# Row factors of the t and s operands as one-hot products on turned columns, in the last stage of a three-stage kernel

## The chip, the cores and the metric

One core of a Trainium2 chip runs the whole program. Times are device microseconds of one execution. The kernel before took 1745.47 us (median of three runs, 1743.71 to 1745.48). TensorE does the matmuls, VectorE (DVE), ScalarE (ACT) and GpSimd (POOL) the elementwise work; SyncE (SP), ScalarE and GpSimd issue DMAs.

## What is computed

Attention-like mixing and a gated MLP come first; they give x1, 4096 tokens of 512 channels. The change lies in the third stage, which conditions each token by table rows and sends it through two layers and a quantised product:

```python
h = _ln(x, pw_g[pathway_ids], pw_b[pathway_ids])
h = _ln(h, cp_g[compartment_ids], cp_b[compartment_ids])
t = _ln(x, tm_g[time_steps], tm_b[time_steps])
m = x + _mlp_ln(memory_state, ...)[:, None, :]      # n and r alike
s = _ln(x, ms_g[scale_type], ms_b[scale_type])
cat = concatenate([w[0]*h, w[1]*t, w[2]*m, w[3]*n, w[4]*r, w[5]*s])
u = _mlp_ln(cat, int_W1, int_b1, int_W2, int_b2, int_g, int_be)
x = x + quantised_product(u, rhs)                   # int8 rows and columns
```

`_ln(x, g, b)` is the layer norm of a token times g plus b. tm_g has 5 rows and ms_g has 3, of 512 channels each; pw_g has 500. The shifts tm_b, ms_b and cp_b and the vectors of m, n and r are already brought in by a small table, `bias_t`, multiplied by a one-hot matrix of the tokens' ids.

## The kernel before

`conditioned_ffn` holds the stage. It runs over eight blocks of 512 tokens (TT = 4 tiles of 128). In each, the first layer is a sum over 16 steps: four steps x (the columns of x1, channel-major, loaded from `x1T_d`), four steps h, then t and s in turn for the four channel groups k. `main(b, s)` on TensorE multiplies four blocks of weights by one operand of 128 channels x 512 tokens, in three passes over high and low parts: 12 matmuls a step (L2085; the last four steps are `main_last`, L2112). The operand's high part is made by ScalarE (`front_high`, L2293, or `x_high`, L2286, for x), its low part by VectorE (`front_low`, L2711), in four slots `op`.

For h, t and s the operand comes from token-major tiles. For t and s a table row per token (`ts_rows`, 1024 numbers) is gathered by GpSimd with an indirect DMA (`gather_ts`, L2537) into `gts`. ScalarE writes the centred x1 into `xh` (`x_centre`, L2302). VectorE multiplies the t half by xh (`t_product`, L2701) and GpSimd the s half (`scale_rows`, L2544). TensorE turns the products, four transposes an operand (L2048), into one bank of a ring of four, and ScalarE and VectorE take their parts from the bank. For h the same is done with `hn`: rows gathered from pw_gb (L2518), multiplied and added on GpSimd (`h_rows`, L2557, L2559), moments on VectorE, rstd and shift on GpSimd (`rsqrt`, L2548, L2550), centring on ScalarE, and a product with cp_rows on VectorE (`h_product`, L2696).

The order on each engine is written out by hand:

- TensorE: the list `order` puts the items (turned operands, q products) between the main steps; then `main_last`; then `second(b)` (L2133), the second layer. `wait_bank` waits until the bank's last content has been read. main(b + 1, 0) waits for `take_u` to have emptied the accumulators.
- ScalarE: 16 steps, then `hidden(b)` (L2361, L2364), then the x operands of the next block. `h_centre(b + 1, [0, 1])` stands in step 15, before `hidden(b)`.
- VectorE: `steps_of(b)` begins with the moments of u of block b - 1; in its steps stand the moments of x and h of block b + 1, `scale` and `clip` of block b - 1 and front_low. Then `hidden(b)` (L2717), front_low of x steps 0 and 1, `h_product(b + 1)`, `take_u(b)` (L2735, waits for each result of the second layer), front_low of x steps 2 and 3.
- GpSimd: `body(b)`: scale_rows(b), two gathers of pw rows, rsqrt of u, `tail_gain(b - 1)` (L2579, L2581: u times a row plus a row), `tokens(b + 1)` (rsqrt of x, h_rows, four gathers of cp_rows, rsqrt of h), tail_add of tiles 0 and 1 (L2587), gather_ts, tail_add of tiles 2 and 3.
- SP: ids, residual rows, the turns of q by DMA, the loads of x1 tiles, the stores of the output.

The blocks are `body(0)`, a loop over pairs for blocks 1 to 6, and `body(7)`.

Of the kernel before, what the change touches and what calls it, by code (L numbers as in the profile page):

```python
# [4 lines left out]
F32 = mybir.dt.float32  # L5
# [90 lines left out]
def adaln_attn_ffn_kernel(nc, ins, out):  # L96
# [5 lines left out]
    x1T_d = nc.dram_tensor("x1T_d", (D, TOK), F32, kind="Internal").ap().rearrange("(k p) t -> p k t", p=P)  # L102

    ctx = ExitStack()
    with ctx:
# [17 lines left out]
        def following(sems, marks):  # L123
            return mlp_half(nc, at, sems, marks, ps, vec, v, ident, ones_r, eps6, ins, xT, hs2_d, x1_d, x1T_d, p_d, out_v)
# [718 lines left out]
def mlp_half(nc, at, sems, att, ps, vec, v, ident, ones_r, eps6, ins, xT, hs2_d, x1_d, x1T_d, p_d, out_v):  # L843
# [87 lines left out]
    ffn = conditioned_ffn(nc, at, cleared, ps, vec, v, ident, ones_r, ins, x1_d, x1T_d, xt, out_v)  # L931
# [750 lines left out]
def conditioned_ffn(nc, at, cleared, ps, vec, v, ident, ones_r, ins, x1_d, x1T_d, xt, out_v):  # L1682
# [55 lines left out]
    sT = small("states_sb", [P, KT, GROUP])  # L1738
    sel = small("group_sum", [P, GROUP])
# [7 lines left out]
    rstd = small("rstds", [P, 3, TT])  # L1747
    sc = small("token_scale", [P, 3, TT])
    shift = small("mean_shift", [P, 3, TT])
# [35 lines left out]
    cp_rows, ts_rows = sem("f_cp_rows"), sem("f_time_scale_rows")  # L1785
# [39 lines left out]
    T_AT = 0  # L1825
    QT_AT, FF_AT = 8, 10
    QT_STEP = [9, 9, 10, 11]
    ABS_AT, W2_AT, PEAK_AT = 5, 8, QT_AT
    PEAK = {0: 1, 2: 2, 3: 3}

    items = []

    def add_items(s):
        o, k = steps[s]
        items.append((FRONT[o], k, ("op_low", NS, s, 0)))

    order = []
    for s in range(NS):
        if s % 2 == 0 and XF <= s + AHEAD < NS:
            for ahead in (AHEAD, AHEAD + 1):  # L1840
                add_items(s + ahead)
                order.append(("item", len(items) - 1))
# [9 lines left out]
    for n in (0, 4):  # L1852
        at_main = next(i for i, x in enumerate(first_order) if x == ("item", n)) + 2
        first_order.insert(at_main - 2, first_order.pop(at_main))
# [8 lines left out]
    FREED = {2: 1, 3: 2, 6: 3, 7: 4}  # L1863

# [9 lines left out]
    def sync_program(sp, mlp):  # L1874
# [9 lines left out]
        def tail(b, nxt2):  # L1884
# [15 lines left out]
            for t in range(1, TT):  # L1900
                turn(t)
# [11 lines left out]
        def body(b, q, nxt, nxt2):  # L1913
            if nxt:
                sp.wait_ge(S["oh_done"], b + 1)
                load_ids(b + 1)
            if isinstance(b, int) and b == 0:
                sp.wait_ge(S["xh_done"], TT * 2)
                load(2)
            else:  # L1920
                tail(b, nxt2)
# [35 lines left out]
        def early():  # L1957
# [4 lines left out]
            for k in range(2, KT):  # L1962
                sp.dma_start(xs_first[:, k - 2], x1T_d[:, k, bass.ts(0, BT)]).then_inc(first_loaded, 16)
            sp.wait_ge(S["xh_done"], TT)
            load(1)
            sp.wait_ge(tab_zero, 1)
            load_ids(0)

# [4 lines left out]
        def prepare():  # L1973
            sp.wait_ge(ts_rows, 16 * TT)
# [6 lines left out]
            sp.wait_ge(S["op_low"], XF)  # L1981
            sp.dma_start(rows[:].rearrange("p r d -> p (r d)"), ins["rows"]).then_inc(ld["rows"], 16)
# [15 lines left out]
    def tensor_program(pe, mlp, bank_at):  # L1998
        def wait_bank(b, n, prev):
# [28 lines left out]
        def item(b, q, n, prev):  # L2028
# [8 lines left out]
            wait_bank(b, n, prev)  # L2037
            emit(b + off, q if off == 0 else 1 - q, n)

        def emit(b, q, n, dst=None):  # L2040
# [3 lines left out]
            if kind in ("th", "tt", "ts"):  # L2044
# [1081 lines left out]
```

## Time and profile before

| | us |
|---|---|
| median of three runs | 1745.47 |
| the profiled execution | 1745.17 |
| its span | 1743.3 |
| the last stage, from the first main step to the end | 1209.55 to 1743.3 |

The page's first part gives each engine's busy time over the span:

```profile
PE 1731.6 (99%) x7935; PEld 1408.6 (81%) x7935; DVE 1192.5 (68%) x1756; ACT 875.4 (50%) x1299; POOL 789.0 (45%) x702
```

The busy time of the first block of the last stage, and of the last block with the end of the program (us from the start, length, then busy us and number of instructions of PE, PEld, DVE, ACT, POOL, the granted clock as a share, the DMA share and GB/s):

```profile
1209.55:1274.79 65.24, 64.38 (x321) 53.03 (x322) 54.50 (x97) 33.42 (x55) 36.68 (x38) 1.00 0.65 227
1661.29:1743.30 82.01, 77.02 (x375) 59.96 (x373) 47.24 (x106) 30.66 (x50) 29.08 (x28) 1.00 0.12 39
```

The granted clock of TensorE is 1.00 in both, its upper level of 2.4 GHz. In a row of instructions in time, "x4" is a run of four of one kind, the second number the time from the start of the first to the end of the last, and a bracket says how long the engine was idle before and what ended that.

### The profile page before, as it was taken

The numbers are of one execution on the slowest core, as the hardware profiler recorded it, in microseconds if no ns is written. First come the engines' busy times: TensorE is split into PE (matmuls) and PEld (weight loads), VectorE is DVE, ScalarE is ACT, GpSimd is POOL, SyncE is SP. The second block draws the span as 40 slices with busy tenths as digits, with TensorE's granted clock in tenths as the row PEclk, the third lists the DMA queues.
The fourth block names the chain that finished last, engine by engine and source line by source line (L and its number), as shares of the span: only waits on it lengthen the run. The fifth ranks groups of instructions, "written<-read, shape, count | busy, mean of one in ns | idle before, by whom it ended". The sixth has DMA issues, their size and how long they took to land. (4 is left out here: it accounts for less than half of the span.)

```text
span 1743.3 us, 23362 instructions
## 1 busy us (share of the span) xinstructions
PE 1731.6 (99%) x7935; PEld 1408.6 (81%) x7935; DVE 1192.5 (68%) x1756; ACT 875.4 (50%) x1299; POOL 789.0 (45%) x702
## 2 busy tenths in 40 slices
PE   9999999999999999999999999999999999999998
PEld 7888888888888888888888888778887787788786
DVE  7766666669989688785563335357886687577565
ACT  7655556565666665674562223243453443443433
POOL 1122221222686566665560000015577877878742
PEclk9999999999999999999999999999999999999999
DMA  6011100120243334222536568877645445544511
GB/s 208 1 49 49 48 21 27 49 73 25 97 142 121 124 103 163 97 97 89 187 136 224 192 199 283 325 253 244 222 138 180 140 161 174 157 158 151 162 47 61
DMA packets 121992, 234.36 MB, mean 134 GB/s; under 512 B 25619, under 2 KB 25875, under 8 KB 121893
## 3 DMA queue, kind: packets, MB, share of 16 engines
q1 hardware_dynamic: 91732, 157.63, 27.1%
q0 software_dynamic: 11776, 41.95, 7.2%
q10 hardware_dynamic: 18384, 33.56, 5.6%
q8 instruction: 50, 0.82, 0.2%
q14 instruction: 50, 0.40, 0.1%
HBM read 170.71 MB, written 58.72 MB: 132 GB/s over the span
## 5 line engine op out<-in xcount | busy, mean ns | idle before, releaser
L1081 PE MATMUL bank<-h_parts,mlp_w 128*128 128x512 f32 x2016 | 459.3, 389 | 0.6 <-ACT product_copy L1301 0.5
L1081 PEld LDWEIGHTS bank<-h_parts,mlp_w 128*128 128x128 f32 x2016 | 378.1, 188 | 80.4 <-ACT product_copy L1301 1.4
L358 PE MATMUL bank<-h_parts,gate_w 128*128 128x512 f32 x1536 | 351.1, 389 | 0.6 <-DVE h_parts L695 0.6
L358 PEld LDWEIGHTS bank<-h_parts,gate_w 128*128 128x128 f32 x1536 | 288.1, 188 | 61.9 <-issue 0.9
L2085 PE MATMUL bank<-operand_parts,int_w 128*128 128x512 f32 x1152 | 279.0, 395 | 0.1
L1146 PE MATMUL bank<-p_parts,mlp_out_w 128*128 128x512 f32 x1152 | 267.4, 391 | 0.0
L1146 PEld LDWEIGHTS bank<-p_parts,mlp_out_w 128*128 128x128 f32 x1152 | 214.7, 188 | 48.0 <-issue 2.5
L2085 PEld LDWEIGHTS bank<-operand_parts,int_w 128*128 128x128 f32 x1152 | 212.5, 188 | 45.5 <-issue 1.7
L620 POOL TENSOR_TENSOR decay_sq<-decay 128x512 f32<-128x512 f32 x32 | 39.2, 1226 | 278.8 <-DVE decay L708 278.8
L1422 POOL TENSOR_TENSOR product_out<-product_out,gelu 128x512 f32<-128x512 f32 x69 | 119.7, 1756 | 96.8 <-DVE product_out L1581 96.2
L1301 ACT ACTIVATE product_copy<-bank,vec_sb 128x512 f32<-128x512 f32 x144 | 99.1, 688 | 106.4 <-PE bank L1081 105.3
L1519 DVE TENSOR_TENSOR p_parts<-p_tile,p_parts 128x512 fp32r<-128x512 f32 x96 | 69.2, 729 | 101.6 <-ACT p_parts L1258 101.6
L1258 ACT ACTIVATE p_parts<-p_tile 128x512 fp32r<-128x512 f32 x96 | 59.7, 630 | 128.9 <-PE bank L1146 109.9
L2548 POOL TENSOR_TENSOR rstds<-rstds,minus_half 128x4 f32<-128x4 f32 x23 | 26.5, 1152 | 185.4 <-DVE mean_shift L2684 184.9
L2293 ACT ACTIVATE operand_parts<-bank 128x512 fp32r<-128x512 f32 x96 | 54.9, 590 | 105.1 <-PE bank L2048 101.5
L2711 DVE TENSOR_TENSOR operand_parts<-bank,operand_parts 128x512 fp32r<-128x512 f32 x96 | 65.3, 684 | 43.3 <-ACT operand_parts L2293 36.7
L2133 PE MATMUL bank<-int_w,hidden_parts 128*128 128x512 f32 x384 | 89.9, 390 | 1.3 <-DVE hidden_parts L2717 0.9
L2112 PE MATMUL bank<-operand_parts,int_w 128*128 128x512 f32 x384 | 90.1, 394 | 0.0
L2133 PEld LDWEIGHTS bank<-int_w,hidden_parts 128*128 128x128 f32 x384 | 71.7, 188 | 18.0 <-issue 2.6
L2112 PEld LDWEIGHTS bank<-operand_parts,int_w 128*128 128x128 f32 x384 | 72.0, 188 | 15.7
L627 POOL TENSOR_TENSOR u<-u,y 128x512 f32<-128x512 f32 x32 | 53.8, 1710 | 59.2 <-DVE u L766 59.2
L1509 DVE TENSOR_TENSOR mlp_w<-raw_mlp_w,mlp_w 128x768 fp32r<-128x768 f32 x42 | 44.3, 1055 | 48.5 <-ACT mlp_w L1234 48.5
(311 smaller groups left out, 2755.8 us busy)
## 6 DMA issues: line engine op xcount, KB each, us to landing
p_tile<-p_d ACTq DMA_DIRECT2D x96, 256.0 KB, 4.9
p_d<-product_out SPq DMA_DIRECT2D x92, 256.0 KB, 2.0
raw_mlp_w<-mlp_gate_g SPq DMA_DIRECT2D x21, 512.0 KB, 3.6
raw_mlp_w<-mlp_fc_g SPq DMA_DIRECT2D x21, 512.0 KB, 4.1
xin<-xT SPq DMA_DIRECT2D x8, 1024.0 KB
hs_d<-u SPq DMA_DIRECT2D x8, 1024.0 KB, 5.0
hs_pair<-hs_d SPq DMA_DIRECT2D x8, 1024.0 KB, 7.6
x_columns<-xT SPq DMA_DIRECT2D x8, 1024.0 KB, 6.7
```

The costliest lines, as they stand in the source:

```text
L358: i = pe.matmul(bank[:], gw[:, w, s, k, m * P:(m + 1) * P], hr[:, q, t, k, :], start=k == 0 and n == 0, stop=k == KT - 1 and n == 2)
L1081: i = pe.matmul(bank[:], wb[g % 2][:, s, w, kk, :], hop[u % 2][o][:, t, kk, :], start=first and kk == 0 and n == 0, stop=kk == 1 and n == ...
L1146: i = pe.matmul(ACC[b % 2][c][:], ow[j // KT][:, s, j % KT, c * P:(c + 1) * P], pr[n % NPR][:, w, :], start=j == 0 and m == 0, stop=j == F ...
L1258: act.activation(pr[n % NPR][:, 0, :], pt[n % NPT][:], ACT.Copy).then_inc(p_high, 1)
L1301: act.activation(dst[:], src[:], ACT.Identity, bias=v(names[g % 2], 2 * VISITS[g // 2][2] + m)).then_inc(done, 1)
L1422: pool.tensor_tensor(po(i)[t][:], po(i)[t][:], gl[t][:], ALU.mult).then_inc(p_mul, 1)
L1519: dve.tensor_tensor(pr[n % NPR][:, 1, :], pt[n % NPT][:], pr[n % NPR][:, 0, :].bitcast(F32), ALU.subtract).then_inc(p_low, 1)
L2085: i = pe.matmul(A[m][:], w1[OPER[o]][:, a, k, m * P:(m + 1) * P], op[:, s % 4, c, :], start=s == 0 and n == 0, stop=False)
L2112: i = pe.matmul(A[m][:], w1[OPER[o]][:, a, k, m * P:(m + 1) * P], op[:, s % 4, c, :], start=False, stop=s == NS - 1 and n == 2)
L2133: i = pe.matmul(A[t][:], zr[:, a, k, t * P:(t + 1) * P], w2[:, c, k, :], start=k == 0 and n == 0 and not ending, stop=k == KT - 1 and n == 2)
L2293: act.activation(op[:, s % 4, 0, :], bank(kind, k)[:], ACT.Copy).then_inc(S["op_high"], 1)
L2711: dve.tensor_tensor(op[:, s % 4, 1, :], x_columns(b, k) if o == "x" else bank(FRONT[o], k)[:], op[:, s % 4, 0, :].bitcast(F32), ALU.subtra ...
```

## The change

The t and s operands are no longer built from gathered rows. A table `gains` holds tm_g and ms_g in high and low parts, in four groups of 32 rows, and TensorE multiplies it by the one-hot matrix: one matmul over 32 rows and 512 columns for each of the eight operands, in place of four transposes. The bank then holds the factor of each channel and token. The centred x is made on columns, `xn`: VectorE multiplies the x columns by the rstd of each token (`x_scaled`), GpSimd adds the shift (`xhat_columns`), and VectorE multiplies the bank by xn (`gain_product`) into SBUF. front_high and front_low read the result there.

For that, each token's rstd and shift are needed in every partition. TensorE turns the 128 x 8 statistics, into the bank in which the turned q of tile 2 would stand (`turn_stats`, after main step 10). ScalarE copies them out (`stats_out`), SP stores them in DRAM and loads them back into all partitions (`store_stats`, `load_stats`). `rstd` and `shift` become one tile `rs`.

The t and s items move in the order: four before main step 6 and four before step 10; before, two before each of steps 6, 8, 10 and 12. The bias group moves from behind step 8 to before step 10. gather_ts, t_product and scale_rows go. In block 0 GpSimd makes both the product and the sum. ScalarE's load_x waits in addition until x_scaled has read the columns.

```diff
@@ order of the items
+    ITEMS_AT = {2: (4, 5), 4: (6, 7), 6: (8, 9, 10, 11), 10: (12, 13, 14, 15)}
+    GAINS_AT = {6: (8, 9), 7: (10, 11), 10: (12, 13), 11: (14, 15)}
+    BIAS_AT = 10
+    FIRST_STAT_QT, FIRST_STAT_AT = 1, 10
+    STAT_QT, STAT_AT = 2, 11
...
@@ SP
+        def store_stats(b):
+            sp.wait_ge(stat_rows_done, b + 1)
+            sp.dma_start(stats_d[b], stat_rows[0:2 * TT, :]).then_inc(stats_stored, 16)
+
+        def load_stats(b):
+            sp.wait_ge(stats_stored, 16 * (b + 1))
+            if b:
+                sp.wait_ge(xn_add, KT * b)
+            for c in range(2):
+                sp.dma_start(spread[:, c, :], stats_d[b:b + 1, c * TT:(c + 1) * TT].rearrange("n t p -> n (t p)").partition_broadcast(P))\
+                  .then_inc(stats_loaded, 16)
...
-            for t in range(1, TT):
-                turn(t)
+            turn(1)
+            turn(2)
+            if nxt:
+                store_stats(b + 1)
+            turn(3)
+            if nxt:
+                load_stats(b + 1)
...
@@ TensorE
+        def turn_stats(b, n, prev):
+            wait_bank(b - 1, n, prev, True)
+            pe.wait_ge(S["x_rs"], 2 * (b + 1))
+            pe.transpose(bank_of[n][0:2 * TT, 0:P], rs[:, XS].rearrange("p c t -> p (c t)"), ident[:]).then_inc(stat_ps, 1)
...
+            elif kind in ("tt", "ts"):
+                if isinstance(b, int) and b == 0:
+                    pe.wait_ge(gain_done, 1)
+                pe.wait_ge(S["oh_done"], b + 1)
+                group, c = gain_of(kind, k)
+                i = pe.matmul(dst[:], gains[group, c, :], oh[group, :], start=True, stop=True, tile_position=(group.start, 0))
...
@@ ScalarE
         def load_x(b, k):
             if k < 2:
                 act.wait_ge(S["op_low"], NS * (b - 1) + k + 3)
+                act.wait_ge(xn_mul, KT * (b - 1) + k + 3)
             else:
                 act.wait_ge(S["op_low"], NS * b + k - 1)
+                act.wait_ge(xn_mul, KT * b + k - 1)
...
+        def stats_out(b):
+            act.wait_ge(stat_ps, b + 1)
+            if not (isinstance(b, int) and b == 1):
+                act.wait_ge(stats_stored, 16 * b)
+            act.activation(stat_rows[0:2 * TT, :], bank("qt", FIRST_STAT_QT if isinstance(b, int) and b == 1 else STAT_QT)[0:2 * TT, 0:P], ACT.Copy).then_inc(stat_rows_done, 1)
...
@@ GpSimd
+        def xhat_columns(b, k):
+            first = isinstance(b, int) and b == 0
+            if first and k < 2:
+                pool.wait_ge(xs_loaded[k], 16)
+            elif first:
+                pool.wait_ge(first_loaded, 32)
+            pool.wait_ge(stats_loaded, 32 * (b + 1))
             if first:
...
+                pool.tensor_tensor(by_tile(xn[:, k]), by_tile(x_columns(b, k)), spread_of(0), ALU.mult).then_inc(xn_mul, 1)
+            pool.wait_ge(xn_mul, KT * b + k + 1)
+            pool.tensor_tensor(by_tile(xn[:, k]), by_tile(xn[:, k]), spread_of(1), ALU.add).then_inc(xn_add, 1)
...
         def body(b, q, prev, nxt):
             if prev:
-                scale_rows(b)
+                for k in range(KT):
+                    xhat_columns(b, k)
...
-            if nxt:
-                for t in range(TT):
-                    gather_ts(b + 1, t, t == 0)
...
@@ VectorE
+        def x_scaled(b, k):
+            dve.wait_ge(S["op_low"], NS * (b - 1) + XF + KT + 2 * k + 2)
+            dve.wait_ge(stats_loaded, 32 * (b + 1))
+            dve.tensor_tensor(xn[:, k], x_columns(b, k), spread[:, 0, :], ALU.mult).then_inc(xn_mul, 1)
+
+        def gain_product(b, s):
+            o, k = steps[s]
+            dve.wait_ge(S[FRONT[o] + "_ps"], KT * b + k + 1)
+            dve.wait_ge(xn_add, KT * b + k + 1)
+            dve.tensor_tensor(source(b, s), xn[:, k], bank(FRONT[o], k)[:], ALU.mult).then_inc(S[o + "_prod"], 1)
...
             if nxt:
                 for s in range(2):
                     front_low(b + 1, s)
+                    x_scaled(b + 1, s)
                 h_product(b + 1)
                 take_u(b)
                 for s in range(2, XF):
                     front_low(b + 1, s)
+                    x_scaled(b + 1, s)
```

## Rows read from the trace of the kernel before

**Rows 1.** Busy by stretch, blocks 1-6: us, PE, PEld, DVE, ACT, POOL

```profile
1274.79:1340.59 65.80, 64.80 (x310) 51.39 (x309) 46.39 (x89) 27.07 (x44) 51.29 (x50) 1.00 0.52 155
1340.59:1405.11 64.52, 64.27 (x309) 51.54 (x308) 46.85 (x89) 27.08 (x44) 51.34 (x51) 1.00 0.50 158
...
1533.20:1597.26 64.06, 64.06 (x310) 51.62 (x308) 45.49 (x89) 27.15 (x44) 50.15 (x50) 1.00 0.50 158
...
sum 386.50, PE 385.25 PEld 309.42 DVE 275.98 ACT 162.52 POOL 304.39; mean PE 64.21 PEld 51.57 DVE 46.00 ACT 27.09 POOL 50.73
```

**Rows 2.** Chain of waits through block 5: start, us, what

```profile
1551.49 0.87 PE bank L2048 x8
...
1558.70 2.74 PE bank L2085 x12
1561.44 0.43 PE bank L2093 x3
1561.87 2.99 PE bank L2085 x12
```

**Rows 3.** Instructions grouped by line, blocks 1 to 6

```profile
L2711 DVE TENSOR_TENSOR operand_parts<-bank,operand_parts 128x512 fp32r<-128x512 f32 x72 | 49.3, 684 | 28.5 <-ACT operand_parts L2293 21.8 <-issue 6.6
...
L2544 POOL TENSOR_TENSOR time_scale_rows<-time_scale_rows,xhat 128x512 f32<-128x512 f32 x27 | 40.5, 1529 | 25.0 <-DMA time_scale_rows<-ts_rows,row_now 25.0
...
L2537 POOL DMA_INDIRECT time_scale_rows<-ts_rows,row_now x24 | 26.3, 1098 | 6.4 <-issue 6.4
...
L2701 DVE TENSOR_TENSOR time_scale_rows<-time_scale_rows,xhat 128x512 f32<-128x512 f32 x24 | 19.4, 851 | 1.0 <-issue 1.0
```

**Rows 4.** Chain of waits at the end of block 2

```profile
1394.66 0.70 DVE hidden_parts L2717
...
1395.50 9.77 PE bank L2133 x42
```

**Rows 5.** GpSimd's instructions in time, blocks 0 and 1: start, us, what

```profile
1234.88 1.80 POOL L2557 TENSOR_TENSOR h_norm<-xhat,pw_rows 128x512 f32<-128x512 f32 x1 [10.27 <-ACT xhat L2302]
...
1275.58 6.03 POOL L2544 TENSOR_TENSOR time_scale_rows<-time_scale_rows,xhat 128x512 f32<-128x512 f32 x4 [6.65 <-DMA time_scale_rows<-ts_rows,row_now]
...
1324.64 0.20 POOL L2550 TENSOR_TENSOR mean_shift<-mean_shift,rstds 128x4 f32<-128x4 f32 x1
```

**Rows 6.** GpSimd's instructions in time, block 2

```profile
1339.93 5.95 POOL L2544 TENSOR_TENSOR time_scale_rows<-time_scale_rows,xhat 128x512 f32<-128x512 f32 x4 [3.40 <-DMA time_scale_rows<-ts_rows,row_now]
...
1349.16 1.38 POOL L2548 TENSOR_TENSOR rstds<-rstds,minus_half 128x4 f32<-128x4 f32 x1
...
1353.19 1.63 POOL L2581 TENSOR_TENSOR u_tiles<-u_tiles,int_rows 128x512 f32<-128x512 f32 x1
...
1365.86 1.30 POOL L2557 TENSOR_TENSOR h_norm<-xhat,pw_rows 128x512 f32<-128x512 f32 x1 [1.73 <-ACT xhat L2302]
...
1377.02 1.30 POOL L2557 TENSOR_TENSOR h_norm<-xhat,pw_rows 128x512 f32<-128x512 f32 x1 [1.88 <-DMA pw_rows<-pw_gb,idx_now]
...
1389.15 0.20 POOL L2550 TENSOR_TENSOR mean_shift<-mean_shift,rstds 128x4 f32<-128x4 f32 x1
...
1397.44 3.01 POOL L2587 TENSOR_TENSOR u_tiles<-u_tiles,x_residual 128x512 f32<-128x512 f32 x2
```

**Rows 7.** GpSimd's instructions in time, block 5

```profile
1530.03 6.02 POOL L2544 TENSOR_TENSOR time_scale_rows<-time_scale_rows,xhat 128x512 f32<-128x512 f32 x4 [2.90 <-DMA time_scale_rows<-ts_rows,row_now]
...
1580.02 0.20 POOL L2550 TENSOR_TENSOR mean_shift<-mean_shift,rstds 128x4 f32<-128x4 f32 x1
```

**Rows 8.** VectorE's instructions in time, end of block 2

```profile
1396.52 2.79 DVE L2711 TENSOR_TENSOR operand_parts<-x_columns,operand_parts 128x512 fp32r<-128x512 f32 x2
1399.23 3.58 DVE L2696 TENSOR_TENSOR h_norm<-h_norm,cp_rows 128x512 f32<-128x512 f32 x4
```

**Rows 9.** VectorE's instructions in time, end of block 4

```profile
1528.22 2.48 DVE L2696 TENSOR_TENSOR h_norm<-h_norm,cp_rows 128x512 f32<-128x512 f32 x4
1531.36 2.73 DVE L2735 TENSOR_TENSOR u_tiles<-bank,int_rows 128x512 f32<-128x512 f32 x4 [0.65 <-PE bank L2133]
```

More of the change, by code:

```diff
@@ L1834, in add_items @@
         o, k = steps[s]
-        items.append((FRONT[o], k, ("op_low", NS, s, 0)))
+        items.append((FRONT[o], k, {"h": ("op_low", NS, s, 0), "t": ("t_prod", KT, k, 0), "s": ("s_prod", KT, k, 0)}[o]))
     order = []
     for s in range(NS):
[L1839 to L1842, printed above, removed]
+        for later in ITEMS_AT.get(s, ()):
+            add_items(later)
+            order.append(("item", len(items) - 1))
         order.append(("main", s))
@@ L1917, in body @@
             if isinstance(b, int) and b == 0:
+                store_stats(1)
+                load_stats(1)
                 sp.wait_ge(S["xh_done"], TT * 2)
@@ L2071, in main @@
             o, k = steps[s]
+            if s == BIAS_AT:
+                if isinstance(b, int) and b == 0:
+                    pe.wait_ge(tab_done, 1)
+                pe.wait_ge(S["oh_done"], b + 1)
+                for m in range(KT):
+                    rows_m = slice(GROUP * m, GROUP * (m + 1))
+                    pe.matmul(A[m][:], bias_t[rows_m, :], oh[rows_m, :], start=False, stop=False, tile_position=(GROUP * m, 0))
             if isinstance(b, int) and b == 0:
@@ L2371, in body @@
                     q_mul(b - 1, s - MUL_AT)
+                if not prev and s == FIRST_STAT_AT:
+                    stats_out(1)
                 if XF <= s + AHEAD < NS:
                     front_high(b, s + AHEAD)
+                if prev and nxt and s == STAT_AT:
+                    stats_out(b + 1)
                 if prev and nxt and XC_AT <= s < XC_AT + 2:
@@ L2682, in moments @@
             dve.wait_ge(S[pre + "_ag"], TT * (b + 1))
-            dve.tensor_scalar(rstd[:, which, :], mv[:, which, :, 1], 1e-5, None, ALU.add).then_inc(S[pre + "_ve"], 1)
-            dve.tensor_scalar(shift[:, which, :], mv[:, which, :, 0], -1.0, None, ALU.mult).then_inc(S[pre + "_ve"], 1)
+            if which == XS and not (isinstance(b, int) and b == 0):
+                dve.wait_ge(stat_ps, b)
+            dve.tensor_scalar(rs[:, which, 0, :], mv[:, which, :, 1], 1e-5, None, ALU.add).then_inc(S[pre + "_ve"], 1)
+            dve.tensor_scalar(rs[:, which, 1, :], mv[:, which, :, 0], -1.0, None, ALU.mult).then_inc(S[pre + "_ve"], 1)
         def x_moments(b, tiles=range(TT)):
```

197 lines of the change are left out of this document (110 added, 87 removed).

## Prediction

> **What bounds the kernel now.** I read the views in this order: busy time by stretch, the chain of waits, then the engines' instructions in time. I call T0 the moment at which TensorE begins a block, and a period the time from one T0 to the next. The change lies in the last stage, eight blocks of 512 tokens. Blocks 1 to 6 take 386.50 us: 65.80 for block 1, 64.52 for block 2, 64.06 for block 5, and the other three share 192.12, 64.04 each [rows 1]. In block 5 TensorE is busy for all of its 64.06 us, while VectorE and GpSimd work 45.49 and 50.15. Whoever stops there takes TensorE for the only bound.
>
> Blocks 1 and 2 say otherwise: TensorE lacks 1.00 and 0.25 us, and at the end of block 2 the chain leaves it for VectorE's hidden_parts [rows 1, 4]. Behind that stands one GpSimd queue per block: the rows scaled for the s operand (L2544), gathers, the rstd of u, eight products and sums, the rstd of x, the h rows, more gathers, the rstd and shift of h (L2550). ScalarE has to centre h with the last of these before it starts hidden(b). Let x be the end of L2544 after T0, and h the end of the last L2550 after T0:
>
> - block 1: x = 1275.58 + 6.03 - 1274.79 = 6.82, h = 1324.64 + 0.20 - 1274.79 = 50.05 [rows 1, 5]
> - block 2: x = 1339.93 + 5.95 - 1340.59 = 5.29, h = 1389.15 + 0.20 - 1340.59 = 48.76 [rows 1, 6]
> - block 5: x = 1530.03 + 6.02 - 1533.20 = 2.85, h = 1580.02 + 0.20 - 1533.20 = 47.02 [rows 1, 7]
>
> From h to the next T0 it is 15.75 and 15.76 us in blocks 1 and 2, twice the same, so GpSimd's queue set those periods. In block 5 it is 17.04: there the queue has 17.04 - 15.75 = 1.3 us of slack, no more. From x to h it is 43.23, 43.47 and 44.17.
>
> **The change part by part.** *TensorE.* The 32 transposes of the t and s operands go: eight take 0.87 [rows 2], so 3.48 us a block. Eight matmuls over 32 rows come, in two groups of four. The nearest row is the bias group, also four matmuls over four row groups. Twelve main matmuls, it, and twelve more take 2.74 + 0.43 + 2.99 = 6.16 us against 5.48 without it, so a group costs 0.68, most of it before and after the four [rows 2]. The second new group stands right before the bias group, so it costs between 0.23 (one main matmul) and 0.68. The transpose of the statistics is one of the 0.11 us kind (0.87 / 8). Removed 3.48, added 0.68 + 0.45 + 0.11 = 1.24: 2.2 us less a block (2.0 to 2.5). If TensorE stayed the bound, a period would be 61.8.
> The Trainium skill (TensorEngine Tiling, "Key Properties") says that tiles run in parallel and that changing the tiling mode drains the engine. The first half alone would give 0.23 a group. The trace's 0.68 for the bias group agrees with the second half, so the page changes nothing on the sum.
>
> *GpSimd.* The four gathers of the t and s rows go (1.10 us each with their gaps [rows 3]); they stand after h and before tail_add of tiles 2 and 3, outside the stretch from x to h. The four products of L2544 (1.53 each, under contention [rows 3]) become four sums of the same size. What matters is when the last of these sums ends. Before, L2544 waited for a gather and could begin before T0. Now sum k waits for VectorE's x_scaled(k), and x_scaled(2) and (3) stand behind take_u, which waits for the end of the second layer, which is T0. Everything GpSimd does for the rest of the block is queued behind them.
>
> *The new x.* In block 4 the four evacuations of take_u end at 1531.36 + 2.73 = 1534.09, 0.89 after T0 [rows 1, 9]. Then come front_low(2), x_scaled(2), front_low(3), x_scaled(3) on VectorE, each 2.48 / 4 = 0.62 (h_product alone, also two operands in SBUF [rows 9]), and two sums on GpSimd of 1.3 (L2557 alone [rows 6]). The two engines hardly overlap on such operands. The same four h_product take 2.48 without GpSimd and 3.58 beside it, and L2544 takes 1.53 instead of 1.3 [rows 3, 6, 8, 9]. So I add them: x = 0.89 + 4 x 0.62 + 2 x 1.3 = 5.97. Whichever of the two engines goes first, the sum is the same. It is 3.1 later than in block 5 and lies between blocks 2 and 1. The period then is 5.97 + 43.35 (mean of blocks 1 and 2) + 15.75 = 65.1.
>
> *A push on take_u.* In block 2 front_low(0) and (1) began at 1396.52 and h_product ended at 1399.23 + 3.58 = 1402.81 [rows 8]. Now eight operations stand there, 4.96 us, and the sums 0 and 1 between them, 2.6: end at 1404.1, or at 1406.7 if both tail_adds (2.6) fall into it as well. In block 2 they did, in part: front_low's two took 2.79 instead of 1.24, beside L2587 at 1397.44 [rows 6, 8]. take_u must begin by 1403.5 (T0 of 1405.11, plus 0.2, less three steps of 0.6). The push is 0.6 to 3.2. Without the gathers of 4.4 us in front of them the tail_adds come earlier, so I stay near the lower end: 1.1. The period: 65.1 + 1.1 = 66.2.
>
> *What may come off or on top.* Off: the centring of x began late in block 2 (1.73 idle at L2557), a product collided with L2581 (1.63 for 1.3), and the transfer behind pw_rows (1.88 idle) may land sooner as 2 MB a block are no longer gathered [rows 6]: 0 to 2.9. On top: front_low of t and s now reads two operands in SBUF instead of the bank (0.68 alone [rows 3]) and can hold up GpSimd's h rows, 0 to 1.0; a tail_add that falls on hidden_parts number 2, 0 to 1.1. I take these as even, since the first part is a loss seen in one block and the last two are not seen at all.
> The Trainium skill (SBUF — State Buffer, "SBUF: two separate sides") says that a VectorE operation with two SBUF inputs and a GpSimd operation that reads SBUF exclude each other for a whole instruction. By it every one of the twelve added or altered VectorE operations a block can cost up to one GpSimd operation; the trace shows such losses for h_product and front_low [rows 8]. That is the last rival below.
>
> *VectorE in the block.* Four products (0.85) go, four x_scaled (0.62) and eight gain products (reading a bank, 0.68) come: 45.5 + 4.5 = 50 of 66 us. TensorE's fourth new matmul waits for a bank that front_low of h3 frees. That stands on VectorE behind scale(1), so behind GpSimd's u rows. I find it 0 to 2 us late, but TensorE now has 66.2 - 61.8 = 4.4 us of room. It costs nothing while the GpSimd queue sets the period, and shows as a stall.
> *Queues.* SP issues store_stats between the third and fourth turn of q and load_stats behind it. These are some 0.4 us each, and behind them wait the last turn and its ff product: inside the same room. The statistics have a trip through DRAM, but 20 us until x_scaled. On ScalarE stats_out waits for TensorE's turned statistics and load_x for xn_mul; both come earlier than their use. All this at nothing, with TensorE's room as cover; 0 to 2 us a block without it.
>
> *Blocks 0 and 7.* No chain of this kind closes over them. Each gives 2.2 less, and I charge 1 each for new waits (eight operations of 1.3 on GpSimd in block 0, covered by its 10.27 us of idle time [rows 5]; scale and the bank wait in block 7): -2.3 together (-4.4 to +2).
>
> **The sum.** The profiled execution took 1745.17 with a span of 1743.3, 0.3 below the median of 1745.47. Blocks 1 to 6: 6 x 66.2 = 397.2 against 386.5, +10.7. Blocks 0 and 7: -2.3. 1745.2 + 8.4 = 1753.6 (own range 1749 to 1760, periods of 65.4 to 67.3).
>
> **The rivals.**
> (a) take_u isn't pushed, as the tail_adds are over and GpSimd's first sums find gaps: periods of 65.0, 390.0, +3.5 - 2.3: 1746.4. For it: in block 2 h_product ended 0.7 us before take_u had to begin (1403.5 - 1402.81). Against: VectorE's eight operations are back to back.
> (b) Faster: the waits inside GpSimd's queue shrink. The gathered rows no longer fill the DMA queues, centring starts at once, no product collides; 65.1 - 1.8 = 63.3 a period, 379.8, -6.7 - 2.3: 1736. It decides from 1.1 us taken off. For it: 1.88 us of wait for pw_rows, 1.73 for xhat [rows 6]. Against: the gathers that go aren't under way when pw_rows are fetched.
> (c) Faster: TensorE stays the bound, since x comes out near block 5's 2.85 after all; 61.8 a period, 370.8, -15.7 - 4.4: 1725. Against it: the order in the code, take_u before x_scaled(2).
> (d) Slower still: all collisions fall in; 68.0 a period, 408.0, +21.5 - 2.3: 1764.
>
> **How the numbers follow.** Forecast 0.44, (a) 0.19, (b) 0.18, (c) 0.09, (d) 0.10. A measurement of this kernel can tell about 0.2% (3.5 us) from no change. Faster: (b), (c): 0.27. Same: (a), 0.19. Slower: forecast and (d), 0.54. The range, 1732 to 1764, leaves out (c) and the outer parts of (b) and (d).
>
> **What would show it.** Right: in the busy time by stretch TensorE falls short of the period by several us in blocks 1 to 6; the last GpSimd sum ends about 6 to 7 us after T0; h lies near 50 and T0 follows it by 15.75; VectorE's take_u begins without waiting for TensorE. The transposes gone, groups of four at 0.43 in their place: right for the 2.2. Wrong: periods near 62 with TensorE full, or x under 4; or TensorE waiting not for hidden_parts but for front_low or the turns of q.

## The result, and the profile after

The changed kernel takes 1765.03 us (median; 1763.54 to 1768.29) against 1745.47: a ratio of 1.0116, 95% interval 1.0098 to 1.0134. It is slower, as forecast, but by 19.6 us where 8.1 were forecast, and 1 us outside the range. The profiled execution took 1763.58 with a span of 1761.7, 18.4 longer than before.

The busy time by stretch, blocks 0, 1, 2, 6, and 7 with the end (columns as in [rows 1]):

```profile
1209.47:1282.03 72.56, 66.28 (x298) 52.49 (x298) 62.66 (x99) 36.05 (x60) 40.38 (x38) 0.95 0.50 166
1282.03:1349.09 67.06, 62.96 (x285) 48.57 (x286) 52.80 (x97) 27.64 (x46) 47.27 (x44) 1.00 0.45 129
1349.09:1416.12 67.03, 62.76 (x286) 48.48 (x287) 52.33 (x97) 27.45 (x45) 47.48 (x44) 1.00 0.45 129
...
1617.61:1682.42 64.81, 62.66 (x285) 48.51 (x285) 52.07 (x97) 27.78 (x45) 47.32 (x44) 1.00 0.42 124
1682.42:1761.70 79.28, 74.25 (x349) 56.82 (x350) 52.27 (x113) 29.90 (x48) 30.02 (x28) 0.99 0.13 41
```

| us | before | after | forecast | difference to the forecast |
|---|---|---|---|---|
| up to block 0 | 1209.55 | 1209.47 | 0 | -0.1 |
| block 0 | 65.24 | 72.56 | 64.1 | +8.5 |
| blocks 1 to 6 | 386.50 | 400.39 | 397.2 | +3.2 |
| block 7 and the end | 82.01 | 79.28 | 80.9 | -1.6 |

(The forecast of -2.3 for blocks 0 and 7 together is split in halves.) The largest error is in block 0, which the sum had dismissed in a sentence.

**Blocks 1 to 6.** Periods of 67.06, 67.03, 67.00, 67.31, 67.19 and 64.81, where 66.2 was forecast. In block 2 TensorE is busy for 62.8 us and idle for 4.3, as against none in block 5 of before [rows 1]. GpSimd's instructions of block 2, which starts at 1349.09 (start, us, what; in brackets the idle time before it and what ended it):

```profile
1354.23 1.28 POOL L2631 TENSOR_TENSOR xhat_columns<-xhat_columns,x_scale_shift 128x512 f32<-128x512 f32 x1 [0.69 <-DVE xhat_columns L2785]
...
1386.93 1.28 POOL L2644 TENSOR_TENSOR h_norm<-xhat,pw_rows 128x512 f32<-128x512 f32 x1 [2.71 <-DMA pw_rows<-pw_gb,idx_now]
...
1399.70 0.20 POOL L2637 TENSOR_TENSOR rstds_and_shifts<-rstds_and_shifts 128x4 f32<-128x4 f32 x1
...
1404.40 1.40 POOL L2674 TENSOR_TENSOR u_tiles<-u_tiles,x_residual 128x512 f32<-128x512 f32 x1 [2.00 <-DMA x_residual<-x_d]
```

So x = 1354.23 + 1.28 - 1349.09 = 6.42, and h = 1399.70 + 0.20 - 1349.09 = 50.81. ScalarE in the same block shows what hangs on h:

```profile
1399.94 1.52 ACT L2374 ACTIVATE h_norm<-h_norm,rstds_and_shifts 128x512 f32<-128x512 f32 x2 [10.85 <-POOL rstds_and_shifts L2637]
1401.37 0.67 ACT L2438 ACTIVATE hidden_full<-bank,vec_sb 128x512 f32<-128x512 f32 x1
```

It waits 10.85 us for GpSimd's last shift, centres two h tiles, and only then starts on the hidden layer. In block 5 of before h ended 17.04 ahead of the next T0 and that wait was covered. VectorE at the end of block 2:

```profile
1405.21 1.93 DVE L2805 TENSOR_TENSOR hidden_parts<-hidden_full,hidden_parts 128x512 fp32r<-128x512 f32 x2 [0.55 <-ACT hidden_parts L2441]
...
1415.18 2.47 DVE L2823 TENSOR_TENSOR u_tiles<-bank,int_rows 128x512 f32<-128x512 f32 x4
```

The last two low parts of the hidden layer take 1.93 together; the first of them takes 1.15 where the others take 0.69, beside tail_add of tile 2 on GpSimd (1404.40). take_u begins without a bracket: it waits for no one, VectorE was late. It ends at 1417.65, 1.53 after T0 (1416.12) where the forecast had counted from 0.89. TensorE's waits in block 2:

```profile
1368.76 0.50 PE L2114 MATMUL bank<-one_hot,gain_table 32*128 32x512 f32 x1 [0.93 <-DVE operand_parts L2800]
...
1390.94 1.02 PE L2126 MATMUL bank<-rhs_q,q_transposed 128*128 128x512 bf16 x4 [1.51 <-DMA q_transposed<-q_tile]
...
1403.53 0.93 PE L2198 MATMUL bank<-int_w,hidden_parts 128*128 128x512 f32 x3 [0.67 <-issue]
1404.81 0.93 PE L2198 MATMUL bank<-int_w,hidden_parts 128*128 128x512 f32 x3 [0.35 <-DVE hidden_parts L2805]
1406.50 9.78 PE L2198 MATMUL bank<-int_w,hidden_parts 128*128 128x512 f32 x42 [0.76 <-ACT hidden_parts L2441]
```

The waits of 0.93 for the bank of the fourth gain product and of 1.51 for the last turned q had been forecast, at no cost; those of 0.67, 0.35 and 0.76 stand at the start of the second layer. Together 4.2 us.

**Block 0.** TensorE there:

```profile
1245.43 0.49 PE L2114 MATMUL bank<-one_hot,gain_table 32*128 32x512 f32 x1 [2.06 <-DVE rhs_peak L3079]
1248.81 0.79 PE L2114 MATMUL bank<-one_hot,gain_table 32*128 32x512 f32 x1 [2.89 <-ACT stat_rows L2394]
...
1249.95 5.29 PE L2158 MATMUL bank<-operand_parts,int_w 128*128 128x512 f32 x12
...
1282.03 1.20 PE L2158 MATMUL bank<-operand_parts,int_w 128*128 128x512 f32 x4 [1.14 <-DVE u_tiles L2823]
```

Two waits of 2.06 and 2.89 us, and then twelve matmuls in 5.29 us that take 2.74 in [rows 2]. The stretches of the same moments show why (us, TensorE's busy time, the granted clock, DMA):

```profile
1245.00:1247.00 2.00, 0.49 (x1) 1.00 0.17 25
1247.00:1249.00 2.00, 0.19 (x4) 0.77 0.67 238
1249.00:1250.00 1.00, 1.00 (x6) 0.50 0.02 4
...
1255.00:1256.00 1.00, 1.00 (x8) 1.00 1.04 397
```

In the second of these waits the granted clock fell to 0.50, the lower level of 1.2 GHz, and stayed there from about 1248.1 to 1254.9. In block 0 of before it was 1.00 throughout.

A third wait, 1.14 us for take_u, stands at the end of the block. The second and the third lead over ScalarE to VectorE:

```profile
1247.45 1.15 ACT L2479 ACTIVATE x_residual<-rhs_peak 128x512 f32<-128x512 f32 x2 [6.58 <-DVE rhs_peak L3082]
...
1276.17 2.94 ACT L2374 ACTIVATE h_norm<-h_norm,rstds_and_shifts 128x512 f32<-128x512 f32 x4 [3.65 <-DVE xhat_columns L2785]
```

ScalarE empties the bank of the turned statistics (`stat_rows`) only behind a step of the preparation of rhs, and had to wait 6.58 us for VectorE before that (6.82 in the kernel before, but there no turned statistics stood in a bank). At the end of the block its second load_x waits until x_scaled has read the columns, and the centring of h and the last step of rhs (L2429), for which take_u of block 0 waits, stand behind it.

VectorE in block 0, first after:

```profile
1214.60 5.19 DVE L3045 SCALAR_TENSOR_TENSOR bias_table<-bias_high,rowid_sb,cond_hidden_rows 20x128 fp32r<-20x128 f32 x4
...
1233.24 0.69 DVE L2791 TENSOR_TENSOR time_columns<-xhat_columns,bank 128x512 f32<-128x512 f32 x1 [3.99 <-PE bank L2114]
```

then before:

```profile
1214.71 1.41 DVE L2948 SCALAR_TENSOR_TENSOR bias_table<-bias_high,rowid_sb,cond_hidden_rows 20x128 fp32r<-20x128 f32 x4
...
1222.66 2.49 DVE L2701 TENSOR_TENSOR time_scale_rows<-time_scale_rows,xhat 128x512 f32<-128x512 f32 x4
```

The bias table (four short instructions) takes 5.19 instead of 1.41, as GpSimd makes its eight products and sums of xhat at that moment:

```profile
1214.24 1.39 POOL L2629 TENSOR_TENSOR xhat_columns<-x_columns,x_scale_shift 128x512 f32<-128x512 f32 x1 [3.77 <-DMA x_scale_shift<-x_stats_d]
...
1223.63 1.29 POOL L2631 TENSOR_TENSOR xhat_columns<-xhat_columns,x_scale_shift 128x512 f32<-128x512 f32 x1
```

And VectorE's products for t and s, which before were made from 1222.66 on in one go, now wait for banks that TensorE fills behind main step 6 (3.99 us idle). From 1233.24 to 1265 VectorE has hardly any idle time left.

### The profile page after: what moved, and what is told of

Read it like the earlier page. It is cut to its first block and busy times, and to the rows that moved or that the text cites. A ratio compares the mean times of both kernels' runs of the same rounds, so it can differ in the third digit from the quotient of the medians.

```text
span 1761.7 us, 23140 instructions
## 1 busy us (share of the span) xinstructions
PE 1722.5 (98%) x7743; PEld 1386.9 (79%) x7751; DVE 1243.6 (71%) x1814; ACT 878.8 (50%) x1307; POOL 775.2 (44%) x670
## 5 line engine op out<-in xcount | busy, mean ns | idle before, releaser
L1259 ACT ACTIVATE p_parts<-p_tile 128x512 fp32r<-128x512 f32 x96 | 59.8, 630 | 129.1 <-PE bank L1147 108.7
L2635 POOL TENSOR_TENSOR rstds_and_shifts<-rstds_and_shifts,minus_half 128x4 f32<-128x4 f32 x23 | 26.4, 1146 | 186.1 <-DVE rstds_and_shifts L2768 185.8
L2631 POOL TENSOR_TENSOR xhat_columns<-xhat_columns,x_scale_shift 128x512 f32<-128x512 f32 x32 | 48.1, 1503 | 62.2 <-DVE xhat_columns L2785 61.9
L1411 POOL TENSOR_TENSOR mlp_w_sums<-raw_mlp_w 128x256 f32<-128x256 f32 x42 | 41.4, 985 | 67.2 <-DMA raw_mlp_w<-mlp_gate_g 65.4
```

The lines of the kernel that those rows point to most:

```text
L1259: act.activation(pr[n % NPR][:, 0, :], pt[n % NPT][:], ACT.Copy).then_inc(p_high, 1)
L2631: pool.tensor_tensor(by_tile(xn[:, k]), by_tile(xn[:, k]), spread_of(1), ALU.add).then_inc(xn_add, 1)
```

## The experiments

T0 and periods are read from TensorE's main matmuls, h from GpSimd's last shift. Each ratio is to executions of the kernel before on the same chip: 1745.47 us for the changed kernel, 1745.37 for first_fix, sums_late, load_late and before_spin, 1745.97 for the others.

| run | us | ratio, 95% interval | block 0 | blocks 1 to 6 | 7 and end |
|---|---|---|---|---|---|
| changed kernel | 1765.03 | 1.0116, 1.0098 to 1.0134 | 72.56 | 400.39 | 79.3 |
| first_fix | 1767.86 | 1.0122, 1.0105 to 1.0139 | 73.92 | 404.00 | 79.4 |
| sums_late | 1758.83 | 1.0076, 1.0059 to 1.0093 | 72.63 | 395.22 | 79.3 |
| load_late | 1755.61 | 1.0057, 1.0037 to 1.0078 | 72.63 | 389.99 | 79.3 |
| before_spin | 1748.98 | 1.0019, 1.0009 to 1.0029 | 65.31 | 389.77 | 82.0 |
| first_items | 1764.54 | 1.0107, 1.0091 to 1.0124 | 69.95 | 400.94 | 79.3 |
| sums_load | 1758.73 | 1.0074, 1.0057 to 1.0091 | 72.56 | 395.82 | 79.3 |
| three | 1755.25 | 1.0072, 1.0044 to 1.0100 | 69.92 | 395.39 | 79.3 |
| before_late | 1744.62 | 0.9991, 0.9981 to 1.0001 | 65.45 | 387.13 | 82.0 |

The time ahead of block 0 varies by up to 3.6 us from run to run, so the stretches tell more than the totals.

The theory was that GpSimd's queue sets the period of blocks 1 to 6, by way of ScalarE's centring of h. The rival was that TensorE's own waits (bank, turned q) or VectorE set it.

**sums_late.** GpSimd's sums 2 and 3 go to where its queue waits for gathered rows.

```diff
             if prev:
-                for k in range(KT):
+                for k in range(2 if nxt else KT):
                     xhat_columns(b, k)
...
                 if t + 2 < TT:
                     gather(b, t + 2)
+                    if sums:
+                        xhat_columns(b - 1, t + 2)
```

> The changed kernel, with GpSimd's third and fourth sums of a block taken out of the place ahead of the first two gathers and put behind the gathers 2 and 3, where its queue waits for the gathered rows. Theory (GpSimd's queue sets the period of blocks 1 to 6, from x through h to the next block's start): rsqrt of x begins about 2 us earlier, the end of rstd and shift of h falls from 50.8 to 48.8 us after the start of the block, the period from 67.1 to about 65.1, the whole by 10 to 12 us to about 1754 us. Rival (TensorE's own stalls, a gain matmul's bank 0.9 and the turned q 1.3 to 1.8, or VectorE, set the period): h comes earlier and the period stays at 66.8 to 67.1, the whole within 2 us of 1765.

Measured: in block 5 rsqrt of u at 7.40 instead of 9.08, h at 49.52 instead of 50.85, period 65.75 instead of 67.19. The six blocks give back 5.2 us, half of what was expected: of the 1.7 us won at the head of the queue, the sums take part back further on. Blocks 1 to 5, in which GpSimd waited 2 us and more for gathered rows, gave back 6.1; block 6, which waited only 0.87 for them, went from 64.81 to 65.74. The direction, and h and the period moving together by 1.3 and 1.4, speak for the theory.

**load_late.** SyncE loads the x rows of two blocks ahead after the statistics.

```diff
             turn(0)
-            if nxt2:
-                sp.wait_ge(S["xh_done"], TT * (b + 2))
-                load(b + 2)
...
             if nxt:
                 load_stats(b + 1)
+            if nxt2:
+                sp.wait_ge(S["xh_done"], TT * (b + 2))
+                load(b + 2)
```

> The changed kernel, with SyncE's load of the x rows of two blocks ahead (1 MB) moved from behind the first turn of q to behind the load of the statistics. Block 6, which has no such load, has a period of 64.81 us, the blocks 1 to 5 have 67.0 to 67.3. Theory (the load stands in the way of the gathered rows for which GpSimd waits, and of the turned q for which TensorE waits): the waits for the gathered rows (2.71 and 1.6 us) and for the turned q (1.3 to 1.8 us) fall to near nothing, the blocks 1 to 5 come to 64.8 to 65.5 us, the whole 8 to 12 us lower, about 1755 us. Rival (block 6 is shorter because x_centre and x_moments of a block after next are missing on ScalarE and VectorE): periods stay at 67.0, the whole within 2 us of 1765.

Measured: periods of 65.09, 65.30, 64.91, 64.93, 64.89, 64.87, as the expectation had them. In block 3 of the changed kernel GpSimd waited 2.35 for gathered rows (2.71 in block 2). In block 3 here, which starts at 1413.35, that wait is gone and one of 1.14 left:

```profile
1448.49 1.30 POOL L2644 TENSOR_TENSOR h_norm<-xhat,pw_rows 128x512 f32<-128x512 f32 x1
...
1452.32 1.27 POOL L2644 TENSOR_TENSOR h_norm<-xhat,pw_rows 128x512 f32<-128x512 f32 x1 [1.14 <-DMA pw_rows<-pw_gb,idx_now]
...
1461.83 0.20 POOL L2637 TENSOR_TENSOR rstds_and_shifts<-rstds_and_shifts 128x4 f32<-128x4 f32 x1
```

h = 1461.83 + 0.20 - 1413.35 = 48.68, 2.1 earlier than after, and the period is 2.1 shorter. Some 1.2 of it is less waiting; the rest is the last product and sum of the h rows, which took 1.73 and 1.79 in the changed kernel and take 1.27 each here. TensorE's wait for the turned q went as well (1.51 to none), so this run alone doesn't tell the two causes apart.

**before_spin.** A dose on GpSimd, in the kernel before: three small powers a block.

```diff
             if prev:
                 scale_rows(b)
+                if nxt:
+                    spin(b)
...
+        def spin(b):
+            for i in range(3):
+                pool.wait_ge(spun, 3 * (b - 1) + i + 1)
+                pool.tensor_tensor(spin_t[:, i:i + 1], mh4[:, 0:1], mh4[:, 0:1], ALU.pow).then_inc(spun, 1)
```

> The kernel before, with three small powers more on GpSimd behind the scaled rows of each of the blocks 1 to 6, ahead of the first gather: a dose of some 3 us (by the rsqrt rows, about 1 us each) at the place where the change puts its sums. Theory of the prediction (the path x to h to next start, 15.75 plus 43.35 plus x, sets the period in blocks 2 to 4, and has 1.3 us of slack in block 5): x rises from 2.9 to 5.3 in block 1's successors to 6 to 8 us, the period by 2 to 3 us a block, the whole by 10 to 16 us, about 1758 us. Rival (TensorE sets the period of the kernel before): no change, 1745 to 1748 us.

Measured: 3.3 us over six blocks, a miss. The dose itself was smaller than expected: the three powers take 1.8 us (2.3 in blocks 2 and 6). And 2.9 of the 3.3 stand in block 1, 68.68 for 65.80. Its h came 1.6 later (51.65 for 50.05 [rows 1, 5]), which alone would make 1.6; but T0 came 17.03 after it, since TensorE was late by itself:

```profile
1318.66 1.71 PE L2062 MATMUL bank<-rhs_q,q_transposed 128*128 128x512 bf16 x4 [1.97 <-DVE operand_parts L2721]
...
1318.90:1322.30 3.40, 3.40 (x14) 0.50 0.11 21
```

It waited 0.54 and 1.97 for front_low, the second time behind a cast of q on ScalarE that had waited 6.18 us for a turn of q (4.00 in the kernel before), and then worked 3.4 us at a granted clock of 0.50; its second layer ran without a wait. The other blocks hid the dose: in block 5 rsqrt of u came 2.5 later (9.51 for 7.04), h 1.5 later (48.52 for 47.02), as GpSimd's waits inside the queue shrank by 1.0, and 1.3 of that 1.5 was slack. The period became 64.29, 0.23 longer. Neither rival holds as written: TensorE sets blocks 3 to 6 of before, and GpSimd takes over once h passes 48.3. Blocks 4 and 5 of this run show that edge: h at 48.92 and 48.52, T0 15.77 later in both, the 15.75 of the prediction.

**first_fix.** Block 0 alone: main step 10 back ahead of the items t3 and s3, and ScalarE empties the bank of the statistics one step earlier.

```diff
+    ahead = first_order.index(("main", 10))
+    first_order.insert(ahead - 2, first_order.pop(ahead))
...
-                if not prev and s == FIRST_STAT_AT:
-                    stats_out(1)
                 if XF <= s + AHEAD < NS:
                     front_high(b, s + AHEAD)
+                if not prev and s == FIRST_STAT_AT - 1:
+                    stats_out(1)
```

> The changed kernel, with block 0 alone reordered: TensorE's main step 10 goes ahead of the items t3 and s3 (as it stood before the change), and ScalarE takes the turned statistics of block 1 out of their bank one step earlier. In the trace of the changed kernel block 0 takes 72.56 us against 65.24, with waits of 2.06 and 2.89 us at the two items ahead of step 10 and a main step 10 that then takes 5.29 us for 12 matmuls. Theory (the order of the first block's items holds the 5 to 7 us): block 0 comes back to 66 to 68 us, blocks 1 to 6 stay at 67.0, the whole is 5 to 6 us under the changed kernel, about 1759 us. Rival (VectorE has too much to do in block 0, whatever the order): the wait comes back at another item, block 0 stays over 71 us and the time at 1764 or more.

Measured: block 0 at 73.92, a miss for the theory and a hit for the rival. TensorE's two waits became one:

```profile
1256.62 1.12 PE L2135 MATMUL bank<-ident_sb,x_residual 128*128 128x128 f32 x4 [8.14 <-DVE time_columns L2793]
1257.39 4.07 PE L2160 MATMUL bank<-operand_parts,int_w 128*128 128x512 f32 x12
```

It ends with VectorE's product for t2. VectorE does the same work in the same order and is as late as in the changed kernel (that product starts 45.0 us after T0 in both); TensorE can only choose where to wait. Again the next twelve matmuls are slow (4.07), at a granted clock of 0.50 until about 1259.7.

The run also holds an experiment that nobody made. In its block 2 the gathered rows came 2.3 us later than in the changed kernel:

```profile
1392.57 1.27 POOL L2646 TENSOR_TENSOR h_norm<-xhat,pw_rows 128x512 f32<-128x512 f32 x1 [5.00 <-DMA pw_rows<-pw_gb,idx_now]
...
1405.36 0.20 POOL L2639 TENSOR_TENSOR rstds_and_shifts<-rstds_and_shifts 128x4 f32<-128x4 f32 x1
```

h is at 1405.36 + 0.20 - 1352.25 = 53.31, and the period 69.56, both 2.5 more than in the changed kernel. T0 follows h by 16.25, as elsewhere.

**first_items.** Block 0: the first two gain products ahead of main step 5.

```diff
+    for n in (4, 5):
+        first_order.remove(("item", n))
+        first_order.insert(first_order.index(("main", 5)), ("item", n))
```

> The changed kernel, with the gain products of the first two t and s columns (items t0 and s0) put ahead of TensorE's main step 5 in block 0, as before the change, and not behind step 6. The run with main step 10 ahead left block 0 at 73.9 us: the wait went to VectorE's gain products of t2. In the trace of the changed kernel VectorE stands idle 3.99 us (from 1229.2) for the first gain bank of block 0 and has no idle time from then to 1265.8. Theory (VectorE's queue holds block 0: its eight products wait for banks that TensorE fills late, so the 5.4 us of products no longer lie in idle time): VectorE is ahead by up to 4 us, block 0 falls from 72.56 to 69 to 70 us, the whole to about 1762. Rival (TensorE's order around the statistics' bank holds it): block 0 stays at 72 to 73 us.

Measured: block 0 at 69.95, as expected. VectorE's first product starts without a wait (first row); on TensorE one of the two long waits is left, and slow matmuls behind it:

```profile
1231.64 0.68 DVE L2794 TENSOR_TENSOR time_columns<-xhat_columns,bank 128x512 f32<-128x512 f32 x1
```

```profile
1249.57 0.50 PE L2117 MATMUL bank<-one_hot,gain_table 32*128 32x512 f32 x1 [2.02 <-ACT stat_rows L2397]
...
1250.22 4.60 PE L2161 MATMUL bank<-operand_parts,int_w 128*128 128x512 f32 x12
```

The total fell by only 0.5 us, since this execution reached block 0 2.4 later and its block 6 took 66.08. 2.6 of the 7.3 us of block 0 are thus found. What is left holds 2.02 for the bank of the turned statistics, which ScalarE empties, 1.9 for the slow clock (4.60 for 2.74), and 1.12 for take_u at the end of the block. So each of the two theories of this run held a part of block 0.

**sums_load, three and before_late.** Both moves of blocks 1 to 6 together; the same with first_items; and, in the kernel before, the load moved behind the four turns of q. The other edits are those above.

> The changed kernel with both: GpSimd's third and fourth sums behind the gathers, and SyncE's load of two blocks ahead behind the load of the statistics. Alone, the first took the period from 67.1 to 65.75 (end of shift of h at 49.4), the second to 64.9 (48.7); in both the next block began 16.2 to 16.3 us behind the shift of h, as in the changed kernel. Theory (GpSimd's queue still sets the period in both): the gains add, h ends at 47.3, the period is 63.5 us, the whole about 1746 to 1748 us. Rival (with the load away TensorE sets the period at 64.9): h ends earlier, the period stays 64.8 to 64.9, the whole 1755 us, and the way from h to the next block grows to 17.5 us.

Measured: the gains don't add. Periods of 65.47 to 65.72 in four blocks, no better than sums_late alone and 0.8 worse than load_late alone. With the load out of the way GpSimd had no wait left in which to hide the sums, which now stand in the chain themselves (block 3, which starts at 1414.26):

```profile
1442.82 1.30 POOL L2631 TENSOR_TENSOR xhat_columns<-xhat_columns,x_scale_shift 128x512 f32<-128x512 f32 x1
...
1449.20 1.30 POOL L2631 TENSOR_TENSOR xhat_columns<-xhat_columns,x_scale_shift 128x512 f32<-128x512 f32 x1
...
1463.54 0.21 POOL L2637 TENSOR_TENSOR rstds_and_shifts<-rstds_and_shifts 128x4 f32<-128x4 f32 x1
```

h = 1463.54 + 0.21 - 1414.26 = 49.49, and T0 16.23 later. The rival's period of 64.9 didn't come either: TensorE waited for no turned q and for hardly any bank (0.50), and the period still was 65.72. TensorE's own waits therefore don't set it. Blocks 1 and 4 took 66.73 and 66.61. In both the clock fell at the start of the second layer, in block 1 from about 1336.7 to 1340.1 and in block 4 so:

```profile
1532.00:1534.00 2.00, 0.94 (x3) 1.00 0.89 300
...
1535.00:1536.00 1.00, 0.65 (x2) 0.50 0.26 98
...
1538.00:1540.00 2.00, 2.00 (x10) 0.99 0.35 131
```

> The changed kernel with three moves: the sums behind the gathers, the load of two blocks ahead behind the load of the statistics, and the first two gain products of block 0 ahead of main step 5. If they add: 3 us less than the run without the third, about 1744 us, as fast as the kernel before; if block 0 isn't held by VectorE's late start, the same time as the run without the third.

Measured: block 0 at 69.92 for 72.56, blocks 1 to 6 at 395.39: the gain in block 0 adds, those of the other blocks are as in sums_load. A missed total, as its base was.

> The kernel before, with the same move of SyncE's load of two blocks ahead, behind the four turns of q. Theory (the load stands in the way of the gathered rows, which only matter where GpSimd's queue sets the period): the periods of blocks 1 and 2 (65.80 and 64.52) fall to 64.0 to 64.5, the others stay at 64.0, the whole 1743 to 1745 us. Rival (the load costs TensorE in every block by the turned q): all six periods fall by 1 us or more, the whole under 1740 us.

Measured: 1744.62, a ratio of 0.9991 (0.9981 to 1.0001). Blocks 1 and 2 came to 64.31 and 64.05, as expected, 2 us in all; block 3 took 66.00, with TensorE waiting 1.78 us for take_u at its end, which no other run shows there. The rows of VectorE and GpSimd tell why:

```profile
1461.57 5.77 DVE L2695 TENSOR_TENSOR h_norm<-h_norm,cp_rows 128x512 f32<-128x512 f32 x4
...
1461.90 6.57 POOL L2543 TENSOR_TENSOR time_scale_rows<-time_scale_rows,xhat 128x512 f32<-128x512 f32 x4 [2.02 <-DMA time_scale_rows<-ts_rows,row_now]
```

GpSimd's scaled rows began 59.8 us after T0, where they began 61.4 after it in block 3 of the kernel before, and so they fell on all four operations of h_product. These took 5.77 for 2.48, and take_u began 3.0 later. Moving the load gained where GpSimd's queue was the bound; in blocks 4 to 6 the periods were 64.13 to 64.48, no shorter than before.

**The rule over all runs.** End of h from T0, and the period:

| run, block | h | period | T0 after h |
|---|---|---|---|
| after, 6 | 48.61 | 64.81 | 16.20 |
| load_late, 5 | 48.64 | 64.89 | 16.25 |
| load_late, 2 | 49.07 | 65.30 | 16.23 |
| sums_late, 5 | 49.52 | 65.75 | 16.23 |
| sums_late, 2 | 49.85 | 66.14 | 16.29 |
| after, 3 | 50.77 | 67.00 | 16.23 |
| first_fix, 2 | 53.31 | 69.56 | 16.25 |

Over 4.7 us of h the distance stays within 0.1. Of the 42 blocks 1 to 6 of the changed kernel and its six variants, 39 lie between 16.19 and 16.34. The exceptions are blocks 1 and 4 of sums_load and block 4 of three, with periods of 66.5 to 66.7 and T0 17.0 to 17.2 after h. In all three the granted clock was 0.50 for 3.4 us at the start of the second layer (in three from about 1530.2 to 1533.6), so that layer took longer. It also fell in block 1 of first_fix, from about 1327.9 to 1331.4, ahead of the second layer, which TensorE then began without a wait; that T0 came 16.30 after h there is no evidence for the link. In the kernel before it fell in block 1 of before_spin, as shown there.

**Not measured.** The run that would break the link has all four h tiles centred behind the hidden layer on ScalarE. It was planned for both kernels, also with q copied and not turned, but gave no result, so it stays open. That ScalarE's order is the link rests on its rows and on the table above; that a period would fall to the 63.6 us of TensorE's work and its bank wait without it is only argued. No version that was run beats the kernel before by more than its interval; three, the best in block 0, and load_late, the best in blocks 1 to 6, are 0.7% and 0.6% slower (by its median three is 0.5% slower; one of its four executions took 1764.11).

## Why the prediction was right and where it was wrong

- **TensorE's own work: about right.** Forecast 2.2 us less a block (2.0 to 2.5). In block 7 with the end, where nothing else is in the way, TensorE's busy time fell from 77.02 to 74.25, 2.8. In block 5 it fell from 64.06 to 62.7 only, with some 0.6 of stretched matmuls at the start of the second layer in it (12.0 us for 11.4 in block 2): 1.9, a little under the range.
- **GpSimd's queue as the bound: right.** TensorE lacks 4.1 to 4.4 us in each of blocks 1 to 5, take_u doesn't wait for TensorE, and T0 follows h.
- **x: right within 0.7.** Forecast 5.97 and 1.1 for the push, 7.1; measured 6.42, since the push was 0.64 and is contained in it. GpSimd's sum 0 and 1 and VectorE's four operations of h_product (3.58 for 2.48) exclude each other as the forecast assumed. The Trainium skill (SBUF — State Buffer, "SBUF: two separate sides") says that a VectorE operation with two SBUF inputs and a GpSimd operation that reads SBUF share a port pair, which whichever starts first holds for the whole instruction; the trace agrees, with front_low and x_scaled at 1.78 and 1.77 where they are 0.68 alone.
- **x to h: 1.0 too short.** Forecast 43.35, measured 44.39. "What may come off or on top" took the waits inside the queue as even. The wait for gathered rows grew instead, from 1.88 [rows 6] to 2.71, and three of the four sums of the h rows took 1.60 to 1.62 where they had taken 1.27 or 1.28: 1.0 in all, the top of what was listed for front_low. Off came 0.6 at the centring of x (1.16 for 1.73), 0.3 at the collision with L2581 and 0.3 at the power ahead of it; two gathers took 0.7 more to issue. The gathered rows came later although 2 MB a block less are gathered: the load of 1 MB of x rows lies on the same transfers, as load_late showed, and block 6, which has no such load, without any edit.
- **h to T0: 0.5 too short.** Forecast 15.75, measured 16.22. It is the tail_add on the third low part of the hidden layer (1.15 for 0.69), listed as 0 to 1.1 and set off against gains.
- Together 6.42 + 44.39 + 16.22 = 67.03 against 66.2: 1.0 and 0.5 more on these two terms, 0.7 less on x. The mechanism was right, the sizes off by 0.8 us a block.
- **Block 0: the failed step.** The sum charged 1 us for all new waits of the block: "eight operations of 1.3 on GpSimd in block 0, covered by its 10.27 us of idle time". They began ahead of that idle time and shortened it to 6.66 us: on GpSimd they are covered. But VectorE stretched beside them (bias table 5.19 for 1.41), and the new order took work out of VectorE's idle time: products that could be made early now wait for banks which TensorE fills late, and TensorE waits for the bank of the statistics, which ScalarE empties still later. -1.15 was forecast, +7.3 came. TensorE's idle time in the block rose from 0.86 (65.24 less 64.38) to 6.28, 4.95 of it in the two waits and 1.14 at the end of the block, and its busy time by 1.9: the slow clock's 2.5 and more, less what the transposes gave back. Two terms that the forecast put at nothing are among these waits: that stats_out and load_x "come earlier than their use". In block 0 they did not, and they stand behind the 2.89 and the 1.14. first_items returned 2.6 us of block 0; the other parts are read from the trace and not undone.
- **Block 7: 1.6 better than forecast.** It gave its full 2.7; the charge for new waits there was not needed.
- **Rival (d)** has the time that came, 1764, but with periods of 68.0 and nothing in block 0. It was no better an account.
- The sentence "it costs nothing while the GpSimd queue sets the period" on the bank wait and the turned q was right: in block 3 of sums_load TensorE waited for no turned q and 0.50 for a bank, and the period still followed h.

## What to carry to other kernels

Cost the first and last turn of a pipelined loop by their own rows, with the same care as the steady blocks: their order is another, their idle time sits elsewhere, and work that was hidden may lose its cover there. Idle time of an engine covers only its own work; where it shares a port, look at what the other engine does at that moment. And before a queue is shortened in one place, look whether the waits further down absorb the gain: they hid part of a dose and part of a saving alike. Work that starts earlier can also fall on another engine's work, as in block 3 of before_late.

## What the runs showed of the hardware

- TensorE stood still for 2.06 and 2.89 us with one matmul between; in the second wait its granted clock fell to 0.50 (1.2 instead of 2.4 GHz) for 6.8 us, and twelve matmuls took 5.29 instead of 2.74. Behind 8.14 us of idle time they took 4.07. In sums_load three waits of 1.43, 0.34 and 0.36 at the start of the second layer came with 0.50 for 3.4 us in block 4, and 42 matmuls took 10.74 instead of 9.8; in block 3 of the same run, with waits of 1.39, 0.34 and 0.75, it stayed at 1.00, and nothing read here tells the two blocks apart. So a wait of TensorE can cost more than its length.
- Four short VectorE instructions over 20 partitions (bias table) took 5.19 us instead of 1.41 beside GpSimd's products: each stood behind about one GpSimd instruction of 1.3.
- In block 2 of first_fix GpSimd waited 2.3 us longer for gathered pw rows than in the changed kernel (5.00 for 2.71), and the period was 2.5 longer.
